# Fetch, second normalisation and projections moved batch by batch into the pairwise block

## The chip, the cores and the metric

The kernel runs on one core of a Trainium2 chip. The metric is the device time of one execution in microseconds (us). TensorE is PE in the profile (PEld its weight loads), VectorE is DVE, ScalarE is ACT, GpSimd is POOL and SyncE is SP.

## The reference, cut to what matters

Four sequences of 512 rows of 256 features (fp32) pass through an attention, a mixture of 64 experts of which each row uses four, a second attention in which each row looks only at the 51 keys that a small network ranks best, and a last linear layer. The change lies between the experts and the second attention:

```python
x = x + _L0_ffn_ref(_layernorm(x, axis=-1), ...)     # routed experts (4 per row) + shared ones
x = x + _L1_attn_ref(_layernorm(x, axis=-1), ...)

def _L1_attn_ref(x, gamma, beta, W1, b1, W2, b2, W3, b3, Wqkv, bqkv, Wout, bout):
    mu, var = mean and variance over the features
    xn = (x - mu) * rsqrt(var + 1e-5) * gamma + beta
    h = einsum('bsd,fd->bsf', xn, W1)                               # 128 features
    pair = relu(h[:, :, None, :] - h[:, None, :, :] + b1)           # every row with every row
    pair = relu(einsum('bijf,gf->bijg', pair, W2) + b2)             # 64 features
    sim = einsum('bijg,og->bijo', pair, W3)[..., 0] + b3[0]         # diagonal set to 0
    _, top_idx = top_k(sim, 51)
    qkv = einsum('bsd,ed->bse', xn, Wqkv) + bqkv                    # 32 heads of 2
    ... softmax attention of each row over its 51 keys, then Wout, bout
    return x + out
```

The input of `_L1_attn_ref` is itself normalised, so x is normalised twice: once into y, which is also the residual, and y once more into the rows of the projections.

## The kernel before, in words

The program is a row of blocks. Inside a block each engine has its own list of instructions, ordered by semaphores; between two blocks all engines meet. x is held in SBUF as 16 tiles of 128 rows (TILES), four to a batch (TB = 4, B = 4).

**experts** (L502). Rows are scattered to slots in DRAM, 64 pairs of experts work on them, and ScalarE's queue stores each pair's result (L825). After the last pair POOL waits for the stores (L649) and fetches, for each tile, four rows per token with four indirect DMAs (L654) into a ring of two tiles, `back`. VectorE adds each of the four, weighted, to x (L790), one after the other; the block ends with the last.

**normalise_and_turn_weights** (L944). VectorE takes the statistics of 16 tiles (L962), finishes them in a chain of small operations with a square root on ScalarE in the middle (L98 to L119, L126), writes y (L965), and does the same once more for y (L969). TensorE transposes the weights beside it, and ScalarE keeps them.

**second_projections** (L1014). Per batch: VectorE normalises four tiles of y into `rows` (L1056), TensorE transposes them (L187, eight transposes), ScalarE scales them into `xt` (L1093), TensorE makes q, k and v (L1122) and h (L1130). ScalarE writes `hneg` and `hplus` from h (L1101, L1102), VectorE writes q (L1080) and k, v (L1076), and SP stores k and v to `kv_rows` in DRAM (L1036). POOL adds y to x (L1046) and sets up constants (L1146 to L1159).

**pairwise_attention** (L1165). 256 steps, 16 for each tile n; step t = 16 n + u takes eight rows of four groups. The first layer is a TENSOR_SCALAR of 128x512 for each of eight rows j: five or six on VectorE (L1237), three or two on ScalarE (L1376). TensorE makes the second layer (L1424, two halves, `products`), ScalarE takes it (L1382, `hidden`), TensorE adds up the third layer of the step before (L1434). `unit1` has R = 4 slots, so VectorE can be at most four steps ahead of TensorE: `first_layer` waits for `products` of step t - 4. `between` places the rest of VectorE's work by steps: at u = 2 of tile n + 1 it waits until ScalarE has copied the similarities of tile n (`sim_out`, L1388), clears the diagonal (L1243) and begins seven rounds of MAX8, FIND_INDEX8 and MATCH_REPLACE8 (u = 2, 3, 5, 9, 10, 11, 15). After each round POOL issues eight indirect DMAs (three after the last), one for each key, 51 for a tile (L1228), into `got[n % 2]`. At u = 4 of tile n + 2 VectorE waits for all of tile n's keys and multiplies them with the query (L1269); the softmax and the sum over the values follow.

**second_output** and **last_layer** end the kernel; nothing in them is changed.

Of the kernel before, what the change touches and what calls it, by code (L numbers as in the profile page):

```python
# [8 lines left out]
F32 = mybir.dt.float32  # L9
# [7 lines left out]
P = 128  # L17
# [484 lines left out]
def experts(k):  # L502
# [13 lines left out]
    combined, gathered = k.sem("e_combined"), [k.sem(f"e_gathered{r}") for r in range(2)]  # L516
    stored = [k.sem(f"e_stored{r}") for r in range(RING)]
    PAD = EXPERTS + 8
    with ExitStack() as local:
# [23 lines left out]
        slot = sb("slot", [P, TILES, TOPK], I32)  # L543
        match = sb("match", [P, TILES, EXPERTS])
        weight = sb("weight", [P, TILES, TOPK])
# [7 lines left out]
        back = sb("back", [P, 2, TOPK, D])  # L553
# [39 lines left out]
        def _(pool):  # L593
# [157 lines left out]
        def _(ve):  # L751
# [192 lines left out]
def normalise_and_turn_weights(k):  # L944


    nc = k.nc
    scaled, turned, ready, normed = (k.sem("w_" + n) for n in ("scaled", "turned", "ready", "normed"))
    R = k.raw
    with ExitStack() as local:  # L950
        s = Statistics(k, "ln2", local)
        wfs = local.enter_context(nc.sbuf_tensor("wwfs", [P, C, D], F32))
        bank = local.enter_context(nc.psum_tensor("wbank", [P, 8, 512], F32))
        block = local.enter_context(nc.Block())

        @block.vector
        def _(ve):
            ve.wait_ge(k.raw_loaded, k.RAW_LOADED)
            for o in range(2):
                ve.tensor_scalar(wfs[:, o, :], R.wf[:, o, :], R.scale[:, o:o + 1], None, ALU.mult).then_inc(scaled, 1)  # L960
            for t in range(TILES):
                ve.bn_stats(s.stats[:, t, :], k.x[:, t, :]).then_inc(s.tile_done, 1)  # L962
            finish_statistics(ve, k, s)
            for t in range(TILES):
                ve.tensor_scalar(k.y[:, t, :], k.x[:, t, :], k.mean[:, t:t + 1], k.rstd[:, t:t + 1],  # L965
                                 ALU.subtract, ALU.mult).then_inc(normed, 1)
            for t in range(TILES):
                ve.wait_ge(normed, t + 1)
                ve.bn_stats(s.stats[:, t, :], k.y[:, t, :]).then_inc(s.tile_done, 1)  # L969
            ve.wait_ge(normed, TILES)  # L970
            finish_statistics(ve, k, s, turn=1)

        odd = lambda w, c: w.rearrange("p (f c) -> p f c", c=C)[:, :, c]

        def turns():
            for c in range(C):
                yield bank[:, 0, c * P:(c + 1) * P], odd(R.w1[:, :], c), P
                yield bank[:, 1, c * P:(c + 1) * P], odd(R.wqk[:, :], c), P
                yield bank[:, 2, c * KW:(c + 1) * KW], odd(R.wv[:, :], c), KW
                yield bank[0:KW, 3, c * P:(c + 1) * P], R.wout[:, c, :], P  # L980
            yield bank[:, 4, 0:KW], R.w2[:, :], KW
            for o in range(2):
                for c in range(C):
                    yield bank[:, 5 + c, o * P:(o + 1) * P], odd(wfs[:, o, :], c), P

        @block.tensor
        def _(pe):
            pe.wait_ge(k.raw_loaded, k.RAW_LOADED)
            pe.wait_ge(scaled, 2)
            for dst, src, rows in turns():  # L990
                mm = pe.transpose(dst, src, k.ident[0:rows, 0:rows])  # L991
            mm.then_inc(turned, 1)

        @block.scalar
        def _(act):
            act.wait_ge(turned, 1)
            pair = lambda b, n: bank[:, b, 0:C * n].rearrange("p (c n) -> p c n", c=C)
            act.activation(k.w1t[:, :, :], pair(0, P), ACT.Copy).then_inc(ready, 1)
            take_root(act, s)

            by_dim = lambda w: w.rearrange("p (h d) -> p d h", d=HD1)
            for c in range(C):
                for src, z in ((bank[:, 1, c * P:c * P + KW], 0), (bank[:, 1, c * P + KW:(c + 1) * P], 1),
                               (bank[:, 2, c * KW:(c + 1) * KW], 2)):
                    act.activation(k.wqkvt[:, c, z * KW:(z + 1) * KW].rearrange("p (d h) -> p d h", d=HD1),
                                   by_dim(src), ACT.Copy).then_inc(ready, 1)
            act.activation(k.woutt[:, :], bank[0:KW, 3, 0:D], ACT.Copy).then_inc(ready, 1)
            act.activation(k.w2t[:, :], bank[:, 4, 0:KW], ACT.Copy).then_inc(ready, 1)
            act.activation(k.wft[:, :, :], bank[:, 5:7, 0:D], ACT.Copy).then_inc(ready, 1)
            take_root(act, s, turn=1)  # L1010
            act.wait_ge(ready, 10)


def second_projections(k):  # L1014


    nc = k.nc
    normed, turned, xt_ready = k.sem("p_normed"), k.sem("p_turned"), k.sem("p_xt_ready")
    h_done, h_ready, qkv_done, qkv_ready = (k.sem("p_" + n) for n in ("h_done", "h_ready", "qkv_done", "qkv_ready"))
    ordered, added = k.sem("p_ordered"), k.sem("p_added")  # L1020
    stored = [k.sem(f"p_stored{r}") for r in range(2)]
    with ExitStack() as local:  # L1022
        def sb(name, shape, dt=F32):
            return local.enter_context(nc.sbuf_tensor("p" + name, shape, dt))
        gamma, beta, b1, bqkv = k.small[:4]
        rows, xt = sb("rows", [P, 2, TB, D]), sb("xt", [P, 2, C, S])
        bias = sb("bias", [P, 3 * KW])
        kv = sb("kv", [P, 2, TB, 2 * KW])
        bank = local.enter_context(nc.psum_tensor("pbank", [P, 8, 512], F32))
        block = local.enter_context(nc.Block())  # L1030

        @block.sync
        def _(sp):
# [624 lines left out]
```

## Time and profile before

| | |
|---|---|
| median of 3 runs | 1988.36 us (1979.6 to 1989.48) |
| the profiled execution: time, span | 1989.22 us, 1987.5 us |
| busy share of the span: PE, DVE, ACT, POOL | 81%, 73%, 62%, 60% |
| fetches and their sums (L654, L790) | 508.2 to 591.9 us |
| second normalisation (L960 to L119) | 595.2 to 616.4 us |
| second projections | 616.9 to 647.0 us |
| 256 steps of the pairs on PE | 649.3 to 1823.5 us |
| gathers of the keys on POOL (L1228) | 726.9 to 1901.9 us |
| last instruction | 1983.8 us |

Times in the profile are counted from the start of the span; the execution's own time is 1.7 us longer than its span. A timeline row says when a run of like instructions began, how long it lasted, which engine and line, what it writes and reads, and in brackets how long the engine sat idle before it and what released it; "issue" is a release that the profile does not show.

### The profile page before, as it was taken

How to read it: one execution, taken by the hardware profiler on the slowest of the kernel's cores; microseconds unless marked ns; L12 is line 12 of the kernel's file. 1: busy time of each engine (PE TensorE's matmuls, PEld its weight loads, DVE VectorE, ACT ScalarE, POOL GpSimd, SP SyncE). 2: the span in 40 equal slices, each digit the busy share in tenths (PEclk: the TensorE clock that was granted, in tenths of full speed). 3: DMA queues.
4: the chain of work that ended last, by engine and by line, in shares of the span. 5: the costliest groups of instructions: out<-in, count | busy, mean ns of one | idle time of the engine just before them, and what ended most of it. 6: DMA issues, size and time to landing. Idle time of an engine off the chain costs nothing. (4 is left out here: it accounts for less than half of the span.)

```text
span 1987.5 us, 34957 instructions
## 1 busy us (share of the span) xinstructions
PE 1614.0 (81%) x13143; PEld 679.5 (34%) x13143; DVE 1450.6 (73%) x2937; ACT 1226.8 (62%) x1707; POOL 1186.6 (60%) x1107
## 2 busy tenths in 40 slices
PE   6997697889105999999999899999899899996025
PEld 3543454666004233233233233233233233232014
DVE  5656532333337666999999889999899889997656
ACT  4554211333002999989889789889789789885001
POOL 0000077665662037777777777777777777777721
PEclk9999698999556999999999999999999999998557
DMA  8400134999430001111111111111111111111201
GB/s 278 150 1 2 48 115 153 351 345 334 123 91 18 6 15 50 45 46 46 46 47 44 46 48 46 46 48 45 49 46 45 46 49 45 47 47 46 53 16 43
DMA packets 98263, 157.35 MB, mean 79 GB/s; under 512 B 23088, under 2 KB 66224, under 8 KB 98096
## 3 DMA queue, kind: packets, MB, share of 16 engines
q0 software_dynamic: 40448, 95.49, 16.5%
q1 hardware_dynamic: 40240, 42.85, 6.4%
q10 hardware_dynamic: 17408, 16.78, 2.5%
q8 instruction: 106, 1.74, 0.4%
q14 instruction: 61, 0.50, 0.1%
HBM read 109.94 MB, written 45.09 MB: 78 GB/s over the span
## 5 line engine op out<-in xcount | busy, mean ns | idle before, releaser
L1228 POOL DMA_INDIRECT sgot<-kv_rows,sat x816 | 926.7, 1136 | 346.8 <-issue 244.7
L1424 PE MATMUL spre<-sunit,w2t 128*32 128x512 f32 x8192 | 943.3, 598 | 57.6 <-DVE sunit L1237 54.6
L1382 ACT ACTIVATE sunit<-spre,b 128x1024 f32<-128x1024 f32 x512 | 570.9, 1115 | 150.2 <-PE spre L1424 150.2
L1237 DVE TENSOR_SCALAR sunit<-hneg,hplus 128x512 f32<-128x512 f32 x1344 | 569.8, 485 | 38.0 <-PE spre L1424 37.8
L1424 PEld LDWEIGHTS spre<-sunit,w2t 128*32 128x32 f32 x8192 | 290.6, 111 | 660.7 <-issue 507.4
L1376 ACT ACTIVATE sunit<-hneg,hplus 128x512 f32<-128x512 f32 x704 | 481.9, 712 | 0.6 <-PEq L1022 0.6
L1434 PE MATMUL ssims<-sunit,bands 128*32 128x512 f32 x2048 | 273.6, 600 | 0.4 <-ACT sunit L1382 0.4
L1269 DVE TENSOR_TENSOR sprod<-sgot,sbeside 128x3264 f32<-128x3264 f32 x16 | 75.1, 4692 | 85.1 <-DMA sgot<-kv_rows,sat 84.9
L1434 PEld LDWEIGHTS ssims<-sunit,bands 128*32 128x32 f32 x2048 | 73.8, 112 | 152.4 <-issue 151.2
L594 POOL MEMSET ebefore<- 128x128 f32 x1 | 0.2, 204 | 195.0 <-POOLq L221 195.0
L814 ACT ACTIVATE epxt<-ebank 128x512 f32<-128x512 f32 x64 | 38.2, 597 | 114.8 <-DVE eyout L783 93.6
L776 DVE TENSOR_TENSOR ephid<-ebank,epsg 128x128 f32<-128x128 f32 x64 | 18.7, 292 | 116.2 <-ACT epsg L821 114.5
L618 POOL DMA_INDIRECT slot_rows<-erows,eslot x64 | 64.3, 1005 | 63.1 <-DVE eslot L709 43.9
L634 POOL DMA_INDIRECT ewd<-L_ffn_wd,edown_rows x64 | 64.6, 1009 | 60.3 <-PE ebank L887 56.3
L1466 PE MATMUL oturned<-ident,ao 128*64 128x128 f32 x16 | 4.0, 419 | 103.8 <-PEq L1185 103.8
L874 PE MATMUL ebank<-epxt,ewgu 128*64 128x128 f32 x1024 | 71.5, 283 | 15.0 <-DMA ewgu<-gate_up 14.6
L654 POOL DMA_INDIRECT eback<-slot_out,eslot x64 | 60.6, 947 | 29.0 <-issue 19.2
L991 PE MATMUL wbank<-ident,w1raw 128*128 128x128 f32 x2 | 0.9, 440 | 91.4 <-DVE wwfs L960 91.4
L1392 ACT ACTIVATE sbeside<-sprod 128x1248 f32<-128x1248 f32 x16 | 19.2, 1203 | 87.9 <-DVE sprod L1284 87.9
L339 DVE TENSOR_REDUCE a0negpeak<-a0scores 128x1 f32<-128x512 f32 x64 | 43.8, 686 | 39.6 <-PE a0scores L460 39.6
L790 DVE SCALAR_TENSOR_TENSOR x<-eback,eweight,x 128x256 f32<-128x256 f32 x64 | 31.0, 485 | 55.6 <-DMA eback<-slot_out,eslot 53.9
L874 PEld LDWEIGHTS ebank<-epxt,ewgu 128*64 128x64 f32 x1024 | 55.7, 138 | 25.0 <-DMA ewgu<-gate_up 19.9
(251 smaller groups left out, 1786.0 us busy)
## 6 DMA issues: line engine op xcount, KB each, us to landing
slot_rows<-blank SPq DMA_DIRECT2D x4, 4096.0 KB, 27.4
ewgu<-gate_up SPq DMA_DIRECT2D x128, 128.0 KB
exin<-slot_rows POOLq DMA_DIRECT2D x64, 256.0 KB, 5.9
slot_out<-eyout ACTq DMA_DIRECT2D x64, 256.0 KB, 5.4
sgot<-kv_rows,sat POOLq DMA_INDIRECT x816
x<-L_attn_x SPq DMA_DIRECT2D x4, 512.0 KB, 5.5
out<-ftmp SPq DMA_DIRECT2D x4, 512.0 KB, 3.1
slot_rows<-erows,eslot POOLq DMA_INDIRECT x64, 2.4
```

Of the source, the lines that this page charges most:

```text
L339: ve.tensor_reduce(negpeak[:, s:s + 1], scores[:, s % 3, :], AX.X, ALU.max, negate=True).then_inc(peak, 1)
L618: pool.indirect_dma_start(out=xs[:, :], out_offset=bass.IndirectOffsetOnAxis(ap=slot[:, t, j:j + 1], axis=0), in_=rows[:, t, :], in_offset ...
L634: pool.indirect_dma_start(out=wd[:, m % RING, :], out_offset=None, in_=down_table, in_offset=bass.IndirectOffsetOnAxis(ap=down_rows[:, m:m ...
L654: pool.indirect_dma_start(out=back[:, t % 2, j, :], out_offset=None, in_=ys[:, :], in_offset=bass.IndirectOffsetOnAxis(ap=slot[:, t, j:j + ...
L874: mm = pe.matmul(bank[e * FE:(e + 1) * FE, GATE_BANKS[m % 2], z * P:(z + 1) * P], wgu[:, r, e, z, c, :], pxt[:, m % 2, e, c, :], start=c = ...
L1228: pool.indirect_dma_start(out=got[:, n % 2, key, :], out_offset=None, in_=k.kv_rows[:, :], in_offset=bass.IndirectOffsetOnAxis(ap=at[:, n ...
L1237: ve.tensor_scalar(out, a, c, 0.0, ALU.add, ALU.max).then_inc(on_vector, 1)
L1269: ve.tensor_tensor(by_key(prod[:, :, :, :]), threes(n, 0, wide=KW), over_keys(query, KW), ALU.mult).then_inc(attend, 1)
L1376: act.activation(out, a, ACT.Relu, bias=c).then_inc(on_scalar, 1)
L1382: act.activation(unit2[:, t % 2, 2 * h:2 * h + 2, :], pre[:, h, :, :], ACT.Relu, bias=b2[:, 0:1]).then_inc(hidden, 1)
L1424: mm = pe.matmul(pre[32 * g:32 * g + 32, h, c % 2, :], k.w2t[:, 32 * (g % 2):32 * (g % 2) + 32], unit1[:, t % R, 2 * c + g // 2, :], start ...
L1434: mm = pe.matmul(simp[32 * c:32 * c + 32, :], bands[:, 32 * u:32 * u + 32], unit2[:, t % 2, c, :], start=u == 0, stop=u == STEPS - 1, skip ...
```

## The change

The fetches leave the block of the experts, and the two blocks behind it go away; their work is written into `pairwise_attention`, by batches. Ahead of step 0 come the fetches of tiles 0 to 3, their sums, batch 0's statistics, its rows, its transposes and its h. Everything else is placed beside steps 0 to 32:

- POOL: the fetches of tiles 4 to 15 follow at once on those of tiles 0 to 3 and on the constants; the ring `back` has four tiles in place of two.
- VectorE: `ahead(ve, t)`, called once in each step, adds up tile t (4 <= t < 16) and takes its statistics (`combine`), finishes batch b's statistics (`spread_of`) at steps 7, 11 and 19, makes its rows and rewrites x (`rows_of`, `add_normalised`) at 10, 18 and 25, and takes q, k and v at 6, 17, 25 and 32.
- TensorE: batch 0's q, k, v at step 2; for batches 1 to 3 the transposes at steps 11, 19 and 26, and h with q, k, v at 13, 21 and 28.
- ScalarE: the roots at 7, 11 and 19, `xt` at 11, 19 and 26, `hneg` and `hplus` at 13, 21 and 28.

The two normalisations are folded: y and its own statistics are not made; one square root of two columns (the variance plus eps, and that times eps plus the variance) gives both, and x becomes x times (1 + 1/std) less mean/std in one operation per tile on VectorE, in place of y and of POOL's sum. The buffers are put into `got[1]`, `prod`, `k.blank` and the PSUM banks `beside`, all unused until tile 1's keys; so POOL's gathers of tile 1 wait until the q, k, v of all batches are taken. `kv_rows` becomes four tensors, one for each batch.

```diff
@@ experts @@
-            for r in range(RING):
-                pool.wait_ge(stored[r], 16 * PAIRS // RING)
-            for t in range(TILES):
-                if t >= 2:
-                    pool.wait_ge(combined, TOPK * (t - 1))
-                for j in range(TOPK):
-                    pool.indirect_dma_start(
-                        out=back[:, t % 2, j, :], out_offset=None, in_=ys[:, :],
-                        in_offset=bass.IndirectOffsetOnAxis(ap=slot[:, t, j:j + 1], axis=0)).then_inc(gathered[t % 2], 16)
...
-            for t in range(TILES):
-                ve.wait_ge(gathered[t % 2], 16 * TOPK * (t // 2 + 1))
-                for j in range(TOPK):
-                    if j:
-                        ve.wait_ge(combined, TOPK * t + j)
-                    ve.scalar_tensor_tensor(out=k.x[:, t, :], in0=back[:, t % 2, j, :], scalar=weight[:, t, j:j + 1],
-                                            in1=k.x[:, t, :], op0=ALU.mult, op1=ALU.add).then_inc(combined, 1)
-            ve.wait_ge(combined, TOPK * TILES)
...
-def normalise_and_turn_weights(k):
...
-def second_projections(k):
...
+BACK = 4
+SPREAD_AT, ROWS_AT, TURN_AT, QKV_AT = (None, 7, 11, 19), (None, 10, 18, 25), (None, 11, 19, 26), (2, 13, 21, 28)
+UNDER_AT, NORM_STEPS = 8, 15
@@ pairwise_attention, POOL @@
+            for r in range(RING):
+                pool.wait_ge(k.slots_stored[r], 16 * PAIRS // RING)
+            for t in range(TB):
+                fetch(t)
+            set_network_up(k, pool)
+            for t in range(TB, TILES):
+                fetch(t)
             for n in range(TILES):
+                if n % TB == 0:
+                    pool.wait_ge(kv_stored[n // TB % 2], 16 * (n // TB // 2 + 1))
+                if n == 1:
+                    pool.wait_ge(qkv_ready, 3 * B)
@@ VectorE @@
+        def combine(ve, t):
+
+            ve.wait_ge(fetched[t % BACK], 16 * TOPK * (t // BACK + 1))
+            for j in range(TOPK):
+                if j:
+                    ve.wait_ge(combined, TOPK * t + j)
+                ve.scalar_tensor_tensor(out=k.x[:, t, :], in0=back[:, t % BACK, j, :], scalar=k.weight[:, t, j:j + 1],
+                                        in1=k.x[:, t, :], op0=ALU.mult, op1=ALU.add).then_inc(combined, 1)
+            ve.wait_ge(combined, TOPK * t + TOPK)
+            ve.bn_stats(stats[:, t, :], k.x[:, t, :]).then_inc(joined, 1)
...
+            for j in range(TB):
+                x = k.x[:, b * TB + j, :]
+                ve.tensor_scalar(x, x, gain[:, j:j + 1], shift[:, j:j + 1], ALU.mult, ALU.subtract).then_inc(updated, 1)
...
+        def ahead(ve, t):
+
+            if TB <= t < TILES:
+                combine(ve, t)
+            for b in range(B):
+                if b and t == SPREAD_AT[b]:
+                    spread_of(ve, b)
+                if b and t == ROWS_AT[b]:
+                    rows_of(ve, b)
+                    add_normalised(ve, b)
+                if t == QKV_AT[b] + 4:
+                    take_qkv(ve, b)
...
         def first_layer(ve, t, j):
+            if j == 0 and t % (TB * STEPS) == 0:
+                ve.wait_ge(h_ready, 2 * (t // (TB * STEPS) + 1))
...
+            for t in range(TB):
+                combine(ve, t)
+            spread_of(ve, 0)
+            rows_of(ve, 0)
+            add_normalised(ve, 0)
             for n in range(TILES + 3):
                 for u in range(STEPS):
+                    if n == 2 and u == 1:
+                        ve.wait_ge(qkv_ready, 3 * B)
...
                     between(ve, n, u, True)
+                    ahead(ve, n * STEPS + u)
                     for j in second[1:]:
@@ ScalarE @@
+                for b in range(1, B):
+                    if t == SPREAD_AT[b]:
+                        take_roots(act, b)
+                    if t == TURN_AT[b]:
+                        take_xt(act, b)
+                    if t == QKV_AT[b]:
+                        take_h(act, b)
@@ TensorE @@
+            turn_weights(pe)
+            turn_rows(pe, 0)
+            make_h(pe, 0)
+            pe.wait_ge(k.network_set_up, 1)
             for t in range(END + 1):
                 if t < END:
                     second_layer(pe, t)
+                for b in range(B):
+                    if b and t == TURN_AT[b]:
+                        turn_rows(pe, b)
+                    if b and t == QKV_AT[b]:
+                        make_h(pe, b)
+                    if t == QKV_AT[b]:
+                        make_qkv(pe, b)
                 if t:
                     third_layer(pe, t - 1)
```

## Rows read from the trace of the kernel before

**Rows 1.** Source line L1228: ns min/median/max, first and last start in us.

```profile
L1228 POOL DMA_INDIRECT sgot<-kv_rows,sat x816: 944/949/4842, 726.9 to 1901.0; - x164
```

**Rows 2.** Stretches with L1228 alone: length, busy us (count), clock, DMA share, GB/s.

```profile
726.90:799.40 72.50, 56.95 (x51) 1.00 0.17 47
799.40:874.80 75.40, 59.90 (x51) 1.00 0.17 46
...
1838.20:1902.20 64.00, 48.41 (x51) 0.50 0.20 52
```

**Rows 3.** Waits, 790 to 1823 us: us in total, times, longest.

```profile
POOL sgot L1228 <- issue: 213.3, 700, 0.3
...
DVE sprod L1269 <- DMA sgot<-kv_rows,sat: 41.8, 12, 6.4
```

**Rows 4.** Timeline where tiles 0, 1 and 2 reach the search.

```profile
724.85 0.29 DVE L1243 TENSOR_TENSOR ssim<-ssim,sbeside 128x128 f32<-128x128 f32 x1 [9.24 <-ACT ssim L1388]
...
726.94 1.03 POOL L1228 DMA_INDIRECT sgot<-kv_rows,sat  x1 [98.48 <-DVE sat L1249]
...
793.51 0.29 DVE L1243 TENSOR_TENSOR wfraw<-wfraw,sbeside 128x128 f32<-128x128 f32 x1 [9.24 <-ACT wfraw L1388]
...
865.25 0.29 DVE L1243 TENSOR_TENSOR ssim<-ssim,sbeside 128x128 f32<-128x128 f32 x1 [1.94 <-ACT ssim L1388]
```

**Rows 5.** Timeline at both ends of the fetches.

```profile
504.37 1.30 ACTq L825 DMA_DIRECT2D slot_out<-eyout  x2
...
508.25 0.94 POOL L654 DMA_INDIRECT eback<-slot_out,eslot  x1 [9.79 <-DMA slot_out<-eyout]
...
512.01 0.95 POOL L654 DMA_INDIRECT eback<-slot_out,eslot  x1 [0.30 <-issue]
...
514.77 2.04 DVE L790 SCALAR_TENSOR_TENSOR x<-eback,eweight,x 128x256 f32<-128x256 f32 x4 [9.50 <-DMA eback<-slot_out,eslot]
...
595.21 0.61 DVE L960 TENSOR_SCALAR wwfs<-wfraw,wscale 128x256 f32<-128x256 f32 x2 [3.32 <-PEq L519]
```

**Rows 6.** Timeline, second normalisation to the pairs' first step.

```profile
595.74 5.32 DVE L962 BATCH_NORM_STATS2 ln2stats<-x 128x6 f32<-128x256 f32 x16
...
603.46 5.25 DVE L965 TENSOR_SCALAR y<-x,mean,rstd 128x256 f32<-128x256 f32 x16
...
616.89 1.64 DVE L1056 TENSOR_SCALAR prows<-y,mean,rstd 128x256 f32<-128x256 f32 x4 [0.53 <-PEq L950]
...
619.81 1.57 ACT L1093 ACTIVATE pxt<-pbank,beta,gamma 128x512 f32<-128x512 f32 x2 [4.57 <-PE pbank L187]
...
626.46 1.11 PE L187 MATMUL pbank<-ident,prows 128*128 128x128 f32 x8
...
627.40 1.88 PE L1130 MATMUL pbank<-pxt,w1t 128*128 128x512 f32 x4
...
629.82 0.68 ACT L1102 ACTIVATE hplus<-pbank,b 128x512 f32<-128x512 f32 x1
...
636.06 2.76 PE L1122 MATMUL pbank<-wqkvt,pxt 128*128 128x192 f32 x16
...
647.97 12.37 DVE L1237 TENSOR_SCALAR sunit<-hneg,hplus 128x512 f32<-128x512 f32 x31
...
649.30 8.77 PE L1424 MATMUL spre<-sunit,w2t 128*32 128x512 f32 x64 [3.50 <-DVE sunit L1237]
```

**Rows 7.** Stretches: length, PE, PEld, DVE, ACT, POOL busy, clock, DMA, GB/s.

```profile
618.50:620.70 2.20, 1.98 (x8) 1.58 (x8) 2.20 (x6) 0.88 (x2) 2.12 (x2) 0.50 0.00 0
627.00:629.00 2.00, 2.00 (x9) 0.98 (x8) 2.00 (x3) 1.45 (x2) 1.45 (x1) 1.00 0.00 0
662.40:714.00 51.60, 51.60 (x484) 15.50 (x480) 26.11 (x64) 46.90 (x59) 0.00 (x0) 1.00 0.00 1
```

**Rows 8.** Source lines L1076 and L126: ns min/median/max, starts.

```profile
L1076 DVE TENSOR_TENSOR pkv<-pbank,pbias x4: 679/692/692, 629.5 to 644.1; 128x512 f32<-128x512 f32 x4
...
L126 ACT ACT_TABLE_LOAD  x4: 1283/1283/1283, 0.8 to 1939.2; - x4
```

More of the change, by code:

```diff
@@ L515, in experts @@
     p_turned, p_kept, p_up, p_out = (k.sem("e_p_" + n) for n in ("turned", "kept", "up", "out"))
[L516 to L517 removed]
+    stored = k.slots_stored
     PAD = EXPERTS + 8
@@ L941 @@
 SEEN_AT, WIDE_AT, BEGUN_AT = 53, 56, 58
-def normalise_and_turn_weights(k):
[L947 to L1011, printed above, removed]
@@ L1204, in pairwise_attention @@
         block = local.enter_context(nc.Block())
+        spare = got[:, 1, :, :].rearrange("p k n -> p (k n)")
+        back = spare[:, 0:4096].rearrange("p (r j d) -> p r j d", r=BACK, j=TOPK)
+        rows = spare[:, 4096:5120].rearrange("p (t d) -> p t d", t=TB)
+        xt = spare[:, 5120:6144].rearrange("p (c s) -> p c s", c=C)
+        bias = spare[:, 6144:6144 + 3 * KW]
+        products_flat = prod[:, :, :, :].rearrange("p t n e -> p (t n e)")
+        kv = products_flat[:, 0:512].rearrange("p (t n) -> p t n", t=TB)
+        wfs = products_flat[:, 512:1024].rearrange("p (c n) -> p c n", c=C)
+        stats = k.blank[:, 0:96].rearrange("p (t n) -> p t n", n=6)
+        half, spread, var, gain, shift = (k.blank[:, a:a + TB] for a in (96, 100, 104, 108, 112))
+        under, std, r0, r1, roots = (k.blank[:, a:a + 2 * TB] for a in (116, 124, 132, 140, 148))
+        gamma, beta, b1, bqkv = k.small[:4]
+        raw = k.raw
+        turn_at = [pre[:, 0, 0, :], pre[:, 0, 1, :], pre[:, 1, 0, :], pre[:, 1, 1, :], simp[:, :],
+                   beside[:, 0:512], beside[:, 512:1024]]
+        own = [beside[:, z * 512:(z + 1) * 512] for z in range(3)]
         def rows_done(split, t, h):
@@ new lines, in rows_of @@
+        def rows_of(ve, b):
+            own_tiles = slice(b * TB, (b + 1) * TB)
+            n = Tally(b, NORM_STEPS, UNDER_AT)
+            ve.wait_ge(rooted, b + 1)
+            ve.reciprocal(r0, std).then_inc(steps, n.up())
+            ve.wait_ge(steps, n.now())
+            ve.tensor_tensor(r1, r0, r0, ALU.mult).then_inc(steps, n.up())
+            ve.wait_ge(steps, n.now())
+            ve.tensor_tensor(r1, r1, under, ALU.mult).then_inc(steps, n.up())
+            ve.wait_ge(steps, n.now())
+            ve.tensor_scalar(r1, r1, -0.5, 1.5, ALU.mult, ALU.add).then_inc(steps, n.up())
+            ve.wait_ge(steps, n.now())
+            ve.tensor_tensor(roots, r0, r1, ALU.mult).then_inc(steps, n.up())
+            ve.wait_ge(steps, n.now())
+            if b:
+                ve.wait_ge(turned, C * b)
+            for j in range(TB):
+                t = b * TB + j
+                ve.tensor_scalar(rows[:, j, :], k.x[:, t, :], k.mean[:, t:t + 1], roots[:, TB + j:TB + j + 1],
+                                 ALU.subtract, ALU.mult).then_inc(normed, 1)
+            ve.tensor_scalar(gain, roots[:, 0:TB], 1.0, None, ALU.add).then_inc(steps, n.up())
+            ve.tensor_tensor(shift, roots[:, 0:TB], k.mean[:, own_tiles], ALU.mult).then_inc(steps, n.up())
+            assert n.n == NORM_STEPS - UNDER_AT
@@ L1614, in build @@
         k.woutt, k.wft = sb("woutt", [KW, D]), sb("wft", [P, C, D])
-        k.kv_rows = nc.dram_tensor("kv_rows", (N, 2 * KW), F32, kind="Internal").ap()
+        k.kv_rows = [nc.dram_tensor(f"kv_rows{b}", (S, 2 * KW), F32, kind="Internal").ap() for b in range(B)]
         k.q = sb("q", [P, TILES, KW])
```

280 lines of the change are left out of this document (155 added, 125 removed).

## The prediction

> **What bounds the kernel now.** I looked first for the work that releases the end. The chain of waits ends in the last layer, which the change leaves alone, so the question is what holds the block of the pairs until it can begin. TensorE looks like the answer with 81% busy, but the gathers of the keys say otherwise. POOL issues 816 of them between 726.9 and 1901.9 us [rows 1], and their idle time is all of one kind, 0.3 us of issue after each [rows 3]: POOL never rests. Alone, late in the block, 51 gathers take 64.0 us, 1.25 each; beside VectorE's work a tile takes 72.5 to 75.4 us, 1.42 to 1.48 each [rows 2]. VectorE waits for the keys of a tile 12 times, 41.8 us together [rows 3]. So from its first gather on POOL sets the pace, and the end comes a fixed time after that gather. What counts is when tile 0's first gather starts, and whether POOL runs dry afterwards.
>
> Ahead of 726.9 another limit holds. In tile 0 TensorE is busy 51.60 of 51.60 us [rows 7]; the sixteen steps between the two hand-overs took 68.66 us, 4.29 each [rows 4], so the stretch is twelve steps of 4.30. VectorE is busy 26.11 in it, 2.18 a step, and ScalarE 46.90, 3.91 a step [rows 7]. So tiles 0 and 1 go at TensorE's pace. And ahead of 647.97, where VectorE begins step 0 [rows 6], everything is a single file: 83.6 us of fetches at POOL's pace, then 21 us of statistics, then 30 us of projections, all four batches through each before the next may begin.
>
> **The lead in.** The experts' last instruction ends at 504.37 + 1.30 = 505.7. A block's change took 3.3 us [rows 5], so the new block begins at 509.0. POOL starts to fetch there, 0.8 us later than before. Its pitch is (512.01 - 508.25) / 3 = 1.25 us; the sixteenth fetch starts at 509.0 + 15 x 1.25 = 527.8 and is there for VectorE 514.77 - 512.01 = 2.8 us later, 530.6 [rows 5]. Four sums of tile 3 take 2.0, its statistics 0.5 with the wait: 533.1. From the last statistics to the first normalised tile it was 603.46 - 601.06 = 2.4; the new chain has two dependent operations more and one free one less, I take 2.7: 535.8. Four tiles of rows 1.64: 537.5. To ScalarE's first xt 619.81 - 618.53 = 1.3, its two xt 1.6: 540.4. h took 1.88 at a granted clock of 1.00 (2.4 GHz) [rows 6, 7]; TensorE will have stood idle and be at 0.50 (1.2 GHz), as it was at 618.5 [rows 7], so 3.8: 544.2. hneg and hplus 1.2: 545.4, step 0 at 545.5. That is **102.5 us** earlier than 647.97. The weights' transposes, the table load of the first root and VectorE's other small work lie under the 20 us of fetches; without that cover they would cost 5 to 8 us.
>
> **What comes back in tile 0.** TensorE's added work is on the path, since it has no slack: batch 0's q, k, v 2.76, batch 1's transposes 1.11, h 1.71 (four records of 1.88 less the tail) and q, k, v 2.76 [rows 6], **8.3** together. TensorE may still be at 0.50 in the first matmuls of step 0, which I put at 1, between 0 and 3 (a step of 4.30 at half the clock would cost 4.3 more, and the first can't be all cold, since the h before it warms).
>
> VectorE gets more. Each of steps 4 to 15 adds four dependent sums at 2.04 / 4 = 0.51 and the statistics, 0.33 and a wait: 2.45. With 2.18 of first layers that is 4.63, just above TensorE's 4.30. Then q, k, v at step 6 (0.69, and two taken at 0.51: 1.7 [rows 8]), the chain of the statistics at 7 and 11 (1.4 each), rows and x at 10 (1.1 + 1.64 + 0.2 + 1.64 = 4.6). Steps 4 to 15 sum to 12 x 4.63 + 9.1 = 64.7 us on VectorE against 12 x 4.30 + 5.6 = 57.2 on TensorE, an excess of 7.5. VectorE starts step 4 at 4 x 2.18 = 8.7 us; TensorE, 1.3 us behind it at step 0, reaches step 4 only at 18.5 + 2.8 = 21.3. A lead of 12.6 less 2.2 for the rows themselves covers the 7.5, though the excess comes in lumps. I take a stall of **2**, bounds 0 (the lead holds) and 10 (it is not there). The fetches of tiles 4 to 15 need not wait: even at 1.48 each, the worst pitch of rows 2, tile 7 lands near 558, when VectorE comes to tile 4 at 556, and from there on four fetches (5.9) race a VectorE step of 5.4 with a start of four tiles.
>
> ScalarE gains 0.2 + 1.6 + 1.2 for each batch, 3.0 beside TensorE's 5.6 and 0.39 of slack in each step: nothing. The roots stand behind batch 0's root and ahead of the first exponential (step 41). The five roots of before needed four loads of 1.28 us [rows 8]: the second in one block, with only copies between, needed none, so I count none here. If each root took one and gave one back, six would be 7.7 us on ScalarE, in part in its slack. The Trainium skill (ScalarE: Activation LUTs, What ACT_TABLE_LOAD costs) puts a switch of tables at about 2.66 us with a drain; six such would be an estimate of 16.
>
> SP gets the same four stores. POOL loses its four sums into x; VectorE's write of x, 1.64 a batch, is counted above. Together: 102.5 - 8.3 - 1 - 2 = **91.2 us** at tile 0's first gather.
>
> **What comes back in tile 1.** TensorE gets two batches more, 2 x 5.6 = 11.2. At step 18 VectorE has just waited 9.24 us for the similarities [rows 4], so it has at most two steps of lead; it then has 1.8 of search, 4.6 of rows and x of batch 2, and at 19 search again and 1.4 of statistics, while TensorE waits for row 5 of those steps: a stall of 3, bounds 0 and 7. The search of tile 1 thus comes 68.7 + 14.2 = 82.9 us after that of tile 0. POOL needs 72.5 for its 51 gathers [rows 2]. Before, the search was there at 793.51 + 2.09 = 795.6 and POOL at 799.4: 3.8 of slack. Now POOL runs dry for 14.2 - 3.8 = **10.4 us**. The wait for all q, k, v ahead of tile 1's gathers is met at step 32, two steps earlier than the search. In tile 2 the search came at 865.25 + 2.09 = 867.3, POOL at 874.8: 7.5 of slack, now 3.7, enough; nothing is lost afterwards, and nothing can be caught up, since POOL is the pace again. From tile 2 on and in the tail the two kernels do the same.
>
> **The sum.** 102.5 - 8.3 - 1 - 2 - 10.4 = 80.8 us. The profiled execution took 1989.2 us (1987.5 of span), 0.9 above the median of 1988.4, so I forecast 1908.4, **1908 us**.
>
> **The rivals.**
>
> *The added work hides (chance 0.07).* If TensorE's additions fell into waits, little but the clock would come back: 102.5 - 4 = 98, 1891 us. For it: the stalls are mine alone. Against it: TensorE's 51.60 of 51.60.
>
> *VectorE becomes the pace of tiles 0 and 1 (0.13).* Its additions are 12 x 2.45 + 4 x 1.7 + 3 x (1.4 + 4.6) = 54 us. If none had cover, 102.5 - 54 - 1 + 3.8 = 51: 1938 us. For it: 4.63 against 4.30, and the lead is one figure worked out from another. Against it: 16 x (4.30 - 2.18) = 34 us of idle VectorE in tile 0 alone, which this case would leave unused.
>
> *VectorE's bursts hold up the fetches, and the kernel gets slower (0.03).* The fetches of tiles 4 to 15 now run beside the first layers. One gather in the rows lasted 4.84 us instead of 0.95 [rows 1], and 51 of them 72.5 where 64.0 do [rows 2]. If each of the 48 lasted as long as the longest, 5.14 with its gap, they would end at 532 + 247 = 779, and tile 15's sum, due at 616, would come 163 later: 1908 + 163 = 2071 us. The case turns at a pitch of (616 + 81 - 532) / 48 = 3.4 us, 2.4 times what tile 0's gathers show. A rule of the Trainium skill (SBUF — State Buffer, SBUF: two separate sides) says that such a VectorE operation locks GpSimd out of its port, so that it can't write descriptors. By that rule, each fetch that meets a burst waits for its end; the trace agrees in the long gathers, but their mean stays at 1.42.
>
> *The shift is as forecast, the pace is not (in the main chance).* Gathers of a tile took from 64.0 to 75.4 us, and their lumps depend on how VectorE's bursts fall. A shift of 0.3 us a tile either way is 5 us.
>
> **How the numbers follow.** The main case has 0.76, the hidden one 0.07, VectorE's pace 0.13, the slower one 0.03, and 0.01 is left for no change. The main case by its own bounds: 0 to 10 for tile 0's stall, 0 to 7 for tile 1's, 0 to 3 for the clock, 5 either way for the pace, 1898 to 1922. The range reaches to the hidden case and halfway into VectorE's: **1893 to 1930**. 0.5% is 10 us, about what a measurement of this kernel can tell from no change. Faster 0.96, same 0.01, slower 0.03.
>
> **What would show it.** Right: first fetch near 509, step 0 near 545, tile 0's first gather near 636, tile 1's about 83 us behind it with a wait of some 10 us on POOL in front, then gathers without a wait to the end, and 64 us again for the last 51. TensorE without long waits in steps 0 to 15. Wrong: a fetch pitch above 1.5 in tile 0; waits of VectorE for fetches; waits of TensorE for the first layer of several us in steps 5 to 20; first gathers of later tiles after a wait. The prediction fails if POOL is not the pace after all, or if VectorE's lead at step 4 is not there.

## The result and the profile after

The changed kernel takes 1899.17 us (median of 4 executions, 1893.93 to 1901.38) where the kernel before takes 1988.05 (4, 1979.6 to 1989.48) beside it: a ratio of 0.9558, 95% interval 0.9524 to 0.9591, 89 us less. Two repetitions, told below, gave 0.9566 [0.9545, 0.9588] and 0.9600 [0.9575, 0.9624], 86 and 80 us less. The forecast was 80.8 less, a ratio of 0.9594, and 1908 us. The profiled execution took 1893.93 us (span 1892.2), 95.3 less than the profiled one of before; single executions of this kernel lie up to 15 us apart, so part of the 95.3 is chance.

The gathers of keys in the changed kernel, by source line (duration in ns, then first and last start in us), and what ended POOL's idle time ahead of them:

```profile
L1072 POOL DMA_INDIRECT sgot<-kv_rows,sat x816: 938/947/3261, 636.0 to 1805.1; - x164
...
  issue: 244.7, 803
  DVE sat L1196: 44.4, 2
```

This answers to [rows 1]. The first gather starts at 636.0 where 726.9 stood. POOL waits for the search twice, 44.4 us together, and for nothing of weight besides. The same gathers in four stretches, as [rows 2]:

```profile
635.90:720.00 84.10, 56.73 (x51) 1.00 0.18 47
720.00:793.10 73.10, 57.63 (x51) 1.00 0.18 46
793.10:1742.40 949.30, 747.18 (x663) 0.98 0.18 47
1742.40:1806.10 63.70, 48.38 (x51) 0.50 0.21 53
```

Tile 0's turn has grown from 72.5 to 84.1 us: POOL is done and waits for tile 1's search. From tile 1 on each turn takes about 73 us, and the last takes 64 again. The timeline of the lead in and of both hand-overs shows where the time is (start, duration, engine, and in brackets the idle time before it and what ended it):

```profile
507.61 1.30 ACTq L803 DMA_DIRECT2D slot_out<-eyout  x2
...
509.39 0.62 DVE L1308 TENSOR_SCALAR sprod<-wfraw,wscale 128x256 f32<-128x256 f32 x2 [0.87 <-PEq L518]
...
511.48 0.94 POOL L1050 DMA_INDIRECT sgot<-slot_out,slot  x1 [9.78 <-DMA slot_out<-eyout]
...
532.98 2.05 DVE L1082 SCALAR_TENSOR_TENSOR x<-sgot,weight,x 128x256 f32<-128x256 f32 x4 [2.45 <-DMA sgot<-slot_out,slot]
...
542.37 3.72 PE L1478 MATMUL sbeside<-sgot,w1t 128*128 128x512 f32 x4 [0.87 <-ACT sgot L1384]
...
547.33 9.99 DVE L1184 TENSOR_SCALAR sunit<-hneg,hplus 128x512 f32<-128x512 f32 x25 [6.19 <-ACT hplus L1391]
...
635.97 0.94 POOL L1072 DMA_INDIRECT sgot<-kv_rows,sat  x1 [32.35 <-DVE sat L1196]
639.77 1.93 PE L1434 MATMUL spre<-sunit,w2t 128*32 128x512 f32 x16 [1.90 <-DVE sunit L1184]
...
645.45 1.92 PE L1434 MATMUL spre<-sunit,w2t 128*32 128x512 f32 x16 [1.18 <-DVE sunit L1184]
...
720.01 0.97 POOL L1072 DMA_INDIRECT sgot<-kv_rows,sat  x1 [12.08 <-DVE sat L1196]
```

Step 0 of the pairs starts at 547.33 instead of 647.97 [rows 6], the first gather 88.64 us behind it. TensorE waits for VectorE's first layer twice after it, 1.90 and 1.18 us. At 720.01 POOL has been dry for 12.08 us. The stretch of tile 0, all engines (length, PE, PEld, DVE, ACT, POOL busy with counts, clock, DMA share, GB/s):

```profile
549.00:634.00 85.00, 84.95 (x740) 30.12 (x736) 74.00 (x194) 72.99 (x95) 42.12 (x36) 0.98 0.23 65
```

TensorE is busy 84.95 of 85.0 us with all the additions beside the steps; VectorE has room left, 74.0 of 85.0.

So the profiled difference adds up like this. Tile 0's first gather: 91.0 us earlier. Tile 0's turn with the wait: 84.0 less 72.5, 11.5 given back, which leaves 79.4 at tile 1's first gather. Tiles 1 to 15, from 799.4 to 1901.9 us before and from 720.0 to 1806.0 now: 1102.5 against 1086.0, 16.5 gained. Behind the last gather: 85.6 against 86.2, 0.6 lost. Together 95.3.

What the 16.5 are made of can be counted in the trace. From tile 1 on 765 gathers follow each other; at 0.947 us and 0.304 of issue each they take 957.3 us. The rest is what gathers lasted beyond 0.947 us, called their stretch from here on: 145.2 us before and 128.7 now. The experiments below left nine more traces with 51 gathers in every tile and the usual first layers, and in each of them tiles 1 to 15 take 957.3 us and the stretch, within 0.5 us. So POOL sets the pace there, and kernels and executions differ by the stretch alone.

### The profile page after: what moved, and what is told of

The parts are those of the page before. It is cut to its first block and busy times, and to the rows that moved or that the text cites. A ratio compares the mean times of both kernels' runs of the same rounds, so it can differ in the third digit from the quotient of the medians.

```text
span 1892.2 us, 34967 instructions
## 1 busy us (share of the span) xinstructions
PE 1620.1 (86%) x13143; PEld 680.8 (36%) x13143; DVE 1444.8 (76%) x2957; ACT 1226.1 (65%) x1709; POOL 1168.1 (62%) x1103
## 5 line engine op out<-in xcount | busy, mean ns | idle before, releaser
L1072 POOL DMA_INDIRECT sgot<-kv_rows,sat x816 | 909.9, 1115 | 292.5 <-issue 244.7
L1444 PEld LDWEIGHTS ssims<-sunit,bands 128*32 128x32 f32 x2048 | 72.5, 111 | 149.3 <-issue 147.7
L615 POOL DMA_INDIRECT slot_rows<-erows,slot x64 | 63.9, 999 | 67.2 <-DVE slot L696 48.0
L1527 PE MATMUL oturned<-ident,ao 128*64 128x128 f32 x16 | 4.0, 418 | 98.6 <-PEq L984 98.6
L1050 POOL DMA_INDIRECT sgot<-slot_out,slot x64 | 69.4, 1085 | 30.6 <-issue 18.8
L1244 DVE TENSOR_TENSOR sprod<-sgot,sbeside 128x1248 f32<-128x1248 f32 x32 | 64.2, 2009 | 0.0
L386 ACT ACTIVATE a0wt<-a0turn 128x512 f32<-128x512 f32 x64 | 38.3, 600 | 39.6 <-PE a0turn L468 39.6
```

The lines of the kernel that those rows point to most:

```text
L615: pool.indirect_dma_start(out=xs[:, :], out_offset=bass.IndirectOffsetOnAxis(ap=slot[:, t, j:j + 1], axis=0), in_=rows[:, t, :], in_offset ...
L1050: pool.indirect_dma_start(out=back[:, t % BACK, j, :], out_offset=None, in_=k.slot_out[:, :], in_offset=bass.IndirectOffsetOnAxis(ap=k.slo ...
L1072: pool.indirect_dma_start(out=got[:, n % 2, key, :], out_offset=None, in_=k.kv_rows[n // TB][:, :], in_offset=bass.IndirectOffsetOnAxis(ap ...
L1244: ve.tensor_tensor(by_key(prod[:, 0:NEAR, half, :]), threes(n, KW + half.start, 0, NEAR), by_key(near), ALU.mult).then_inc(attend, 1)
L1444: mm = pe.matmul(simp[32 * c:32 * c + 32, :], bands[:, 32 * u:32 * u + 32], unit2[:, t % 2, c, :], start=u == 0, stop=u == STEPS - 1, skip ...
```

## The experiments

Ratios are to the kernel before on the same chip; its medians were 1970.03, 1973.2 and 1981.46 us on the three chips of the timed runs. A comparison of two changed kernels goes by their ratios, times some 1975 us. Where the changed kernel itself did not run beside them, its three ratios stand for it, 0.9558, 0.9566 and 0.9600, and give a range.

**The four tables.** The change also splits the keys' table into one for each batch. Could this be what made tiles 1 to 15 shorter? The kernel before, with that edit alone:

```diff
-        k.kv_rows = nc.dram_tensor("kv_rows", (N, 2 * KW), F32, kind="Internal").ap()
+        k.kv_rows = [nc.dram_tensor(f"kv_rows{b}", (S, 2 * KW), F32, kind="Internal").ap() for b in range(B)]
...
-                            in_offset=bass.IndirectOffsetOnAxis(ap=at[:, n % 2, key:key + 1], axis=0),
-                            element_offset=(n // TB) * S * 2 * KW).then_inc(gathered[n % 2][r], 16)
+                            in_offset=bass.IndirectOffsetOnAxis(ap=at[:, n % 2, key:key + 1], axis=0)).then_inc(gathered[n % 2][r], 16)
```

> The kernel before, with one part of the change alone: kv_rows as four tensors, one for each batch, and no element offset in the gathers. Behind tile 1's first gather the profiled execution of the changed kernel took 1022.4 us for 14 tiles of gathers where the one of before took 1038.9, 16.5 us less, which my sum did not have. Theory A (the tables make a gather cheaper): a tile of gathers is 1.2 us shorter, the time is 1971 us, 17 below before. Theory B (the pitch is set by how VectorE's bursts fall among the gathers, and differs from run to run): no difference, 1988 us within 0.5%, and 71 to 76 us a tile.

Measured: 1970.26 us beside 1970.03, ratio 0.9991 [0.9969, 1.0013]. The 17 us of theory A are excluded; the interval leaves 6 us less to 3 more. Tiles 1 to 14 took 70.1 to 77.0 us each, a little wider than expected, and tiles 1 to 15 together 1086.7 us, as few as in the changed kernel.

**All sums ahead of the pairs.** The changed kernel, with the sixteen sums of the experts' results before step 0, so that only the normalisation and the projections of batches 1 to 3 stay beside the steps:

```diff
-            if TB <= t < TILES:
-                combine(ve, t)
...
-            for t in range(TB):
+            for t in range(TILES):
                 combine(ve, t)
```

> The changed kernel with one part undone: all 16 tiles are fetched and added up ahead of step 0; the statistics, rows and projections of batches 1 to 3 stay beside the steps. Theory A (beside the steps the sums cost nothing, VectorE's lead covers them): step 0 starts 12 x 5.0 = 60 us later and everything behind it too, 1959 us. Theory B (the sums beside the steps slow tile 0): less than that comes back, since tile 0 gets faster without them, by up to 10 us: 1949 us.

Measured: 1954.08 us, ratio 0.9894 [0.9851, 0.9937], 58 to 66 us over the changed kernel by its three ratios. The timeline at step 0 and at the first gather:

```profile
611.19 12.54 DVE L1182 TENSOR_SCALAR sunit<-hneg,hplus 128x512 f32<-128x512 f32 x31 [6.31 <-ACT hplus L1389]
...
699.83 0.94 POOL L1072 DMA_INDIRECT sgot<-kv_rows,sat  x1 [104.71 <-DVE sat L1194]
```

From the first fetch (513.23) to step 0 it is 98.0 us instead of 35.9, and from step 0 to the first gather 88.64, as in the changed kernel's first profile to the hundredth (a later profile of it has 89.34). So twelve of the sixteen fetches and their sums are worth 62 us ahead of the pairs and cost nothing beside them. This also settles VectorE's load in tile 0: taking 27 us of it away (46.6 of 85.0 us busy instead of 74.0) moves nothing. The kernel before needs 139.7 us from the first fetch to step 0, so the other 41.8 us come from the folded normalisation, the three batches that moved and the blocks that went; no experiment told these apart.

**Fewer gathers.** The changed kernel, leaving out the last three of the 51 keys from tile 2 on (the attention then reads old rows for them):

```diff
+    issued = lambda n, r: 0 if n >= 2 and r == ROUNDS - 1 else COUNTS[r]
...
-                    for e in range(COUNTS[r]):
+                    for e in range(issued(n, r)):
```

> The changed kernel without the last three gathers of each tile from tile 2 on (48 for 51); those three keys keep what an older tile left, so the output is not the reference's. Theory A (POOL's queue of gathers is the pace of the pairs): 3 x 1.43 = 4.3 us less for each of 14 tiles, 60 us, until TensorE's 68.7 us a tile or VectorE's 68.8 are met; as 48 x 1.43 = 68.6 lies just there I expect 40 to 60 less, 1840 to 1860 us. Theory B (TensorE or VectorE is the pace and POOL only happens to be busy): less than 5 us of gain, 1895 to 1900.

Measured: 1853.27 us, ratio 0.9405 [0.9378, 0.9432], 30 to 38 us under the changed kernel, less than the 40 to 60 expected. Below are POOL's wait on the search (us in total, times, longest) and the engines' busy times in the pairs' middle stretch:

```profile
POOL sgot L1073 <- DVE sat L1197: 23.2, 10, 3.6
```

```profile
795.10:1702.80 907.70, 887.62 (x8224) 296.25 (x8215) 894.60 (x1709) 819.79 (x1008) 695.88 (x624) 1.00 0.18 47
```

42 gathers fewer are worth less than their 1.43 us each (60): POOL now waits for the search ahead of ten tiles. VectorE is busy 894.6 of 907.7 us, TensorE 887.6. POOL was the pace, but the next floor lies only some 3 us a tile below it: 69.8 us where the changed kernel has 73.0. Whether that floor is VectorE or TensorE, the shares of 98.6% and 97.8% do not tell.

**More gathers.** The other side: two gathers more in each tile from tile 2 on, into space that is free by then.

```diff
+    issued = lambda n, r: 5 if n >= 2 and r == ROUNDS - 1 else COUNTS[r]
...
+                        to = got[:, n % 2, key, :] if key < KEEP else (raw.w1, raw.wqk)[n % 2][:, (key - KEEP) * 128:(key - KEEP + 1) * 128]
+                        key = min(key, KEEP - 1)
```

> The changed kernel with two gathers more for each tile from tile 2 on (53 for 51), into memory that nobody reads. Theory A (POOL's queue is the pace, it has no slack): 2 x 1.43 = 2.9 us more for each of 14 tiles, 36 to 40 us, 1935 to 1939 us. Theory B (POOL is busy but others are the pace): under 10 us more, since POOL's share beyond TensorE's 68.7 us would be slack.

Measured: 1917.57 us, ratio 0.9746 [0.9707, 0.9786], 29 to 37 us over the changed kernel; 28 gathers at 1.25 to 1.43 us are 35 to 40. In the trace POOL waits in these tiles for its own issue and hardly for anything else. By the timed ratios more gathers cost most of their price, fewer give back half of theirs or a little more: POOL sets the pace, narrowly. The profiled execution gives them less: tiles 2 to 15 took 1026.3 us, 14 to 22 more than in the three profiles of the changed kernel.

**The changed kernel once more, and batch 2's rows two steps earlier.** VectorE's burst for batch 2 collides with the search of tile 0 at steps 18 and 19, where the prediction put a stall of 3 us. The edit moves it ahead of the search:

```diff
-    SPREAD_AT, ROWS_AT, TURN_AT, QKV_AT = (None, 7, 11, 19), (None, 10, 18, 25), (None, 11, 19, 26), (2, 13, 21, 28)
+    SPREAD_AT, ROWS_AT, TURN_AT, QKV_AT = (None, 7, 11, 17), (None, 10, 16, 25), (None, 11, 19, 26), (2, 13, 21, 28)
```

> The changed kernel once more, unaltered, so that the others of this group have it on their chip. Theory A (the gain of 89 us is the shift of 91 to 95 us less 4 to 10 that differ by the waits for keys in each execution): ratio to the kernel before 0.955 to 0.960, and first gathers of tiles 0 and 1 84.0 us apart, as in its first profile. Theory B (a part of the gain belongs to one chip): a ratio outside of that, 0.962 or more.

> The changed kernel with two numbers altered: VectorE makes the rows of batch 2 at step 16 in place of 18, and finishes the statistics of batch 3 at step 17 in place of 19, both ahead of its wait of 8.6 us for tile 0's similarities. Theory A (TensorE's waits of 1.90 and 1.18 us at steps 18 and 19 come from these 6 us of VectorE's work, and TensorE is the pace until tile 1's search): both waits go, the first gathers of tiles 0 and 1 are 80.9 us apart for 84.0, POOL's wait ahead of tile 1 is 9 us for 12, and the time is 3 us less. Theory B (the work only moves TensorE's wait to step 16 or 17, or TensorE's extra work alone sets it): 84 us apart as before, or tile 0's first gather 3 us later.

Measured: the changed kernel 1887.5 us, 0.9566 [0.9545, 0.9588], its first gathers 84.05 us apart, as theory A had it; with the rows earlier 1885.71, 0.9555 [0.9535, 0.9575]. The hand-overs with the rows earlier:

```profile
636.70 0.97 POOL L1072 DMA_INDIRECT sgot<-kv_rows,sat  x1 [32.35 <-DVE sat L1196]
...
717.24 0.97 POOL L1072 DMA_INDIRECT sgot<-kv_rows,sat  x1 [10.83 <-DVE sat L1196]
```

Tile 0's turn is 80.5 us instead of 84.1: the two stalls, 3.1 us together, are gone from the trace as expected, and POOL waits 10.8 us, 13.6 in the changed kernel on this chip. The time moves by 2.2 us, which the intervals can tell neither from nothing nor from 3.5. The mechanism is shown, its price isn't.

**A warm TensorE.** As above, and eleven matmuls on spare data ahead of the first transposes, to have the clock at 1.00 for batch 0's h.

```diff
+            for _ in range(11):
+                pe.matmul(own[2], k.ident[:, :], raw.wf[:, :, :].rearrange("p c n -> p (c n)"), start=True, stop=True)
             turn_rows(pe, 0)
```

> The same as the one with early rows, and with eleven matmuls of no use (128 x 512, result not read) on TensorE between the second sum of batch 0's tiles and its transposes, so that TensorE is not at 1.2 GHz when batch 0's rows come. Theory A (the h of batch 0 took 3.72 us at a granted clock of 0.50 where it takes 1.88 at 1.00, and the transposes of one half 1.2 where they take 0.6): from the first fetch to step 0 33.4 us for 35.9, and the time 2.5 us below the kernel with early rows alone, 5 to 6 below the changed kernel. Theory B (TensorE falls back to 0.50 in the wait, or the extra matmuls end late and hold the transposes): 35.9 or more.

Measured: 1883.71 us, 0.9537 [0.9510, 0.9564], not to be told from 0.9555. Stretches of the trace show why:

```profile
534.00:540.40 6.40, 6.40 (x16) 2.52 (x14) 3.46 (x14) 0.21 (x1) 5.44 (x11) 1.00 0.27 78
542.90:549.50 6.60, 5.73 (x12) 2.73 (x12) 1.47 (x6) 1.55 (x2) 4.92 (x6) 0.50 0.37 103
```

The clock came up to 1.00 in the dummies. TensorE then waited 2.42 us for the last normalised rows, and when the transposes began, at 542.88, it stood at 0.50 again. h took 3.78 us, as cold as without them, and first fetch to step 0 took 35.87 us, where the changed kernel has 35.85.

**Twice the projections.** The changed kernel computes q, k and v of batches 1 to 3 twice, 2.76 us more of TensorE at steps 13, 21 and 28 each. It ran once, and then several times beside the changed kernel once more.

```diff
+                        if b:
+                            make_qkv(pe, b, False)
                         make_qkv(pe, b)
```

> The changed kernel with the q, k, v matmuls of batches 1, 2 and 3 done twice, 2.76 us more of TensorE each. Theory A (TensorE has no slack in tiles 0 and 1 and its additions are paid in full): tile 0's first gather 2.8 us later after step 0 (91.4 for 88.6), tiles 0 and 1 89.5 us apart for 84.0, POOL's wait 5.5 longer, 17.5 us. Theory B (VectorE's additions are what is paid): 88.6 and 84.0 stay within 1 us.

> The changed kernel with the q, k, v matmuls of batches 1 to 3 done twice, timed. The single execution had its first gathers 2.6 and 7.8 us later after step 0 and yet took 1888.1 us, as long as the changed kernel's median. Theory A (the loss in tiles 0 and 1 stays): 8 us more than the changed kernel beside it, ratio to before 0.960 to 0.961. Theory B (it is got back in the tiles behind): the same ratio as the changed kernel, within 0.0015.

> The changed kernel unaltered, beside the two others on the same chip: ratio 0.956 to 0.957 by its two measurements so far. If the tiles 1 to 15 really take less than those of the kernel before (1086 and 1078 us in its profiles against 1102 and 1087), a third profile is again at or below 1086; if that was chance, it is as likely above.

The hand-overs in the single execution:

```profile
641.52 0.94 POOL L1072 DMA_INDIRECT sgot<-kv_rows,sat  x1 [34.93 <-DVE sat L1196]
...
730.79 1.24 POOL L1072 DMA_INDIRECT sgot<-kv_rows,sat  x1 [17.38 <-DVE sat L1196]
```

Step 0 (550.29) to the first gather is 91.2 us instead of 88.6, and tile 0's turn 89.3 instead of 84.1, with 17.4 us of wait instead of 12.1: TensorE's additions come through almost whole, 2.6 of 2.8 us in tile 0 and 5.2 of 5.5 in tile 1. Yet the time hardly follows: 1905.36 us, 0.9608 [0.9587, 0.9628], beside 1901.47 and 0.9600 [0.9575, 0.9624] for the changed kernel, 1.6 us more by the ratios and 3.9 by the medians, where 8 went in. The intervals leave anything from nothing to 8 open. The changed kernel's ratio lies outside the 0.956 to 0.957 expected of it; its tiles 1 to 15 took 1079.4 us, under 1086 as expected. But the kernel with twice the projections took 1070.4 us for them in the single execution and 1092.2 in the profile of the timed ones, so one profile of each kernel cannot tell kernels apart here.

**TensorE late in the kernel before.** Thirteen dummy matmuls in tile 1 of the kernel before put POOL's wait there without anything else of the change: 11 us more of TensorE, less 3.8 of slack.

```diff
+                for _ in range({21: 7, 28: 6}.get(t, 0)):
+                    pe.matmul(beside[:, 0:512], k.ident[:, :], k.hneg[:, 0:S], start=True, stop=True)
```

> The kernel before with thirteen matmuls of no use (128 x 512, 0.85 us each) on TensorE in tile 1, seven at step 21 and six at step 28: 11.1 us, as much as the changed kernel has there. It delays tile 1's search and nothing else. Theory A (what POOL loses in tile 1 stays lost, as my sum had it): POOL's wait ahead of tile 1 is 11.1 less 3.8 of slack, and the time 7 us more, 0.4%. Theory B (the tiles behind get it back, since VectorE's waits for keys and the gathers' waits for VectorE's bursts shrink when POOL has no lag): tile 1 starts 7 us late, the time is within 3 us of before, and the tiles from 2 on take less than those of the kernel before.

```profile
813.72 1.03 POOL L1228 DMA_INDIRECT sgot<-kv_rows,sat  x1 [9.96 <-DVE sat L1249]
```

Measured: 1992.82 us, ratio 1.0050 [1.0027, 1.0072], 5 to 14 us more. POOL waited 9.96 us, more than the 7.3 expected, and tile 0's turn took 80.5, where the two other traces with the old layout have 72.5 and 69.3. What POOL loses in tile 1 stays lost here.

**Short first layers.** What sets POOL's pace beyond its own 1.25 us a gather? The changed kernel, with VectorE's first layer on 64 of the 512 columns from tile 2 on (the pairs' similarities are then computed from old columns):

```diff
+            if t >= 2 * STEPS:
+                out, a = out[:, 0:64], a[:, 0:64]
```

> The changed kernel with VectorE's first layer cut to 64 of its 512 columns from tile 2 on (the other columns keep older rows, so the output is not the reference's): as many instructions, each about 0.1 us for 0.41. Theory A (what makes 51 gathers take 72.5 us and more where 63.6 do is VectorE's runs of these instructions, which keep the gathers waiting): the gathers of a tile fall from 57.7 us of busy time to 49 to 51, POOL then has gaps because TensorE with its 68.7 us a tile is the pace, and the time is 14 x (73.0 - 68.7) = 60 us less, about 1835. Theory B (the gathers are slowed by their transfers or by VectorE's other work): they stay above 55 us of busy time a tile; POOL stays without gaps only if they stay near 57.

Its one execution took 2657.27 us and the kernel before beside it 2721.28, some 750 us more than the changed kernel and the kernel before take elsewhere, for a reason that the record does not show. In this trace VectorE and ScalarE sat idle for long stretches that no other trace has, and a tile took about 118 us. So theory A's 60 us are not tested; only the durations of gathers can be read. By source line:

```profile
L1072 POOL DMA_INDIRECT sgot<-kv_rows,sat x816: 938/944/1858, 716.7 to 2569.1; - x164
```

And of the changed kernel:

```profile
802.43 2.07 POOL L1072 DMA_INDIRECT sgot<-kv_rows,sat  x1 [0.30 <-issue]
...
802.73 1.65 DVE L1184 TENSOR_SCALAR sunit<-hneg,hplus 128x512 f32<-128x512 f32 x4
```

With the short layers the mean gather takes 963 ns instead of 1115, and the longest 1858 instead of 3261; the stretch in tiles 2 to 14 is 9.0 us, and 119.3 in the changed kernel. This does not show that the length of the first layers did it. The first 48 gathers of tile 0 ran beside first layers of full length in this same execution, and they already averaged 992 ns, where the same 48 took 1113 in the changed kernel: most of the drop goes with the slow pace, in which the first layers stand further apart.

The trace of the changed kernel says by itself what stretches the gathers. In tiles 2 to 14, 443 of the 663 gathers overlap a first layer of VectorE; they take 1217 ns on average and hold the whole stretch. The other 220 take 946 ns, though VectorE works beside most of them too, on tensor_tensor, reductions and the search. In the kernel before it is 422 gathers with 1263 ns against 241 with 948. The gather shown above meets a run of four first layers and ends at 804.50, 0.12 us behind that run; 36 of the 57 gathers over 1.5 us end at that distance. So the long gathers come from runs of tensor_scalar and not from VectorE's work as such. The Trainium skill (SBUF — State Buffer, Who interferes with whom) says that tensor_scalar can take the port pair that GpSimd needs for descriptors, while tensor_tensor has no such mode; both halves agree with the traces here, by these means. What a shorter or a sparser run would save at full pace is not shown.

## Why the prediction was right

**POOL is the pace from its first gather on: right, and narrowly so.** More gathers cost most of their price, a wait of POOL in tile 1 stays, and VectorE never waited for the fetches of tiles 4 to 15. What the prediction didn't see is how near the next floor is: at 69.8 us a tile VectorE or TensorE would take over.

**The lead in: forecast 102.5 us, measured 100.6 in absolute times.** The experts ended 3.24 us later in this execution than in that of before (507.61 against 504.37), which is no part of the change. From the experts' last store to the first fetch it is 3.9 us in both, so the block's change, charged at 0.8, was hidden. From the first fetch to step 0: 35.85, forecast 36.5. The cold h took 3.72, forecast 3.8.

**Tile 0: forecast 91.2 us at the first gather (near 636), measured 91.0 (635.97).** By parts the hit is partly luck. Step 0 to the first gather grew from 78.97 to 88.64 us, 9.7 instead of 11.3. TensorE's additions (8.3) are there, and twice the projections for batch 1 came through as 2.6 more. That leaves 1.4, which looks like the 1 us put down for the clock and is not. Step 0 had the clock at 0.50 for a while, but so it had in the kernel before, the first of these two stretches (length, PE, PEld, DVE, ACT, POOL busy with counts, clock, DMA share, GB/s); the second is of the changed kernel:

```profile
650.10:653.50 3.40, 3.40 (x20) 0.84 (x16) 3.40 (x9) 3.40 (x7) 0.00 (x0) 0.50 0.01 2
```

```profile
549.30:552.70 3.40, 3.40 (x23) 1.08 (x16) 3.40 (x10) 3.40 (x6) 2.79 (x3) 0.50 0.29 81
```

TensorE's step 1 began 5.15 us behind its step 0 before and 5.39 now, so the clock cost 0.2 us more here, and 1.0 in the repetition (6.12); where the remaining 1.1 went stays open. The stall of 2 on VectorE was not there: TensorE was busy 84.95 of 85.0. This and the block change, 2.8 together, made up for most of the later end of the experts.

**Tile 1: forecast 10.4 us dry, measured 11.8** (12.08 with the usual 0.3). Tile 0's turn is 84.1 where 82.9 was the distance of the searches. The stall of 3 at steps 18 and 19 was 1.90 and 1.18, and went away when batch 2's rows were moved.

**Tiles from 2 on "the same": the term in which the profiles differ most.** Tiles 1 to 15 took 1102.5 us before and 1086.0 after in the first two profiled executions, 16.5 us outside what the sum held, three times the 5 it allowed. How much of this belongs to the change is not shown. Three traces with the old layout have 1102.5, 1086.7 and 1093.3; eight of changed kernels have 1070.4 to 1092.2, with means of 1094 and 1081. But four of these eight ran on a chip on which the old layout was not profiled, and side by side on one chip the difference was 1.8 us once (four tables against all sums first) and 13.9 and 1.1 the other time (TensorE late against the changed kernel and against twice the projections). The timed gains of 80 to 89 us, beside some 83 at tile 1's first gather when the experts' later end is left out, leave between 3 lost and 6 gained. The four tables are not the cause. What differs is the stretch of the gathers, 112.6 to 145.2 us in these eleven traces; why it differs, from kernel to kernel and between two executions of one kernel, stays open. Whether a wait of POOL in tile 1 is partly caught up behind it is open as well: the single execution with twice the projections speaks for it, the timed ones and the kernel before with TensorE late against it.

The forecast of 1908 us counts 80.8 down from the profiled 1989.2; from the median it is 1907.6, which changes nothing.

**The rivals.** "The added work hides" (1891 us) falls, though the profiled time lies near it: the additions are all there, in POOL's wait and in TensorE's busy time. "VectorE is the pace of tiles 0 and 1" falls by TensorE's 84.95 of 85.0 and by the sums placed first. "Bursts hold up the fetches" falls as a price, not as a mechanism: batch 0's fetches came 1.25 us apart and those of batches 1 to 3, beside the first layers, 1.37 to 1.40, the longest of them 3.66; that is far from the 3.4 us at which the case turns, and VectorE waited for none of tiles 4 to 15. The roots, with no table load of their own after the first (one at 515.2 us), went as forecast.

## What to carry to other kernels

Work that stands ahead of a pipeline in single file can go beside its first steps, and is free there on each engine that isn't their pace: here 62 us of fetches and sums cost nothing, while nearly every microsecond that TensorE got was paid for in tiles 0 and 1. Ask where the queue that sets the pace later runs dry, count the slack at each hand-over, and place the bursts clear of the search; here that took 3.5 us out of tile 0's turn, though not provably out of the time. Find how far the next engine is from taking over before you cut the one that leads: three gathers fewer of 51 gave back 30 to 38 us where 60 were taken out. And compare a term between two kernels by more than one profile of each: one kernel here took 1070.4 and 1092.2 us for the same fifteen tiles.

## What the hardware showed

In the warm TensorE's run TensorE was busy with dummies until 540.4 us, the last 6.4 us at a granted clock of 1.00, waited 2.42 us, and had 0.50 (1.2 GHz) when it began again, so warming it up ahead of that wait gave nothing: 35.87 us on the path against 35.85. Gathers that overlap VectorE's tensor_scalar of 512 columns take 1217 ns on average and up to 3261, the others 946; this stretch is 119.3 us of POOL's time in 13 tiles, and in eleven traces it alone makes the fifteen tiles last 1070 to 1103 us. The kernel before had medians from 1970 to 1988 us in four measurements, three of them on different chips, 0.9%, so only ratios on one chip can be compared.
